# A gated cross-attention and expert layer: the first two groups' k, q and v ahead of the slots, and the order inside a slot

## The chip, the cores and the metric

One core of a Trainium2 chip runs the whole kernel. The metric is the device time of one execution in microseconds (us); lower is better. PE is TensorE, DVE is VectorE, ACT is ScalarE, POOL is GpSimd, SP is SyncE, which only issues DMAs here.

## The reference, cut to what matters

```python
def reference(x, ctx, g_xattn, g_ffn, wq, wk, wv, Wr, br, W1, b1, W2, b2):
    # x (64, 128, 128), ctx (64, 77, 128); 16 heads of depth 8; 8 experts of width 256
    def xattn(q, k, v):
        Q, K, V = split(q @ wq.T), split(k @ wk.T), split(v @ wv.T)
        attn = softmax(einsum('bhqd,bhkd->bhqk', Q, K) / sqrt(8))
        return merge(einsum('bhqk,bhkd->bhqd', attn, V))
    def ffn(x):
        logits = x @ Wr + br
        gates = softmax(where(one of the two largest, logits, -inf))
        h = relu(einsum('btd,edh->bteh', x, W1) + b1)
        return einsum('bte,bteh,ehd->btd', gates, h, W2) + gates @ b2
    x = x + tanh(g_xattn) * xattn(layernorm(x), ctx, ctx)
    return x + tanh(g_ffn) * ffn(layernorm(x))
```

The two layer norms have no weights. Only the two chosen experts of a row count.

## The kernel before, in words

Each engine has a program of its own, written out by hand; semaphores (`wait_ge`, `then_inc`) order the engines among each other, and within an engine the order of the program is the order of the work. The program is a loop over **slots** `t` = 0 to 103, and in slot `t` each engine does a piece for several sequences that are at different stages. There are 64 sequences `b` in 16 groups `g` of four (`NB` = 4); `u` = `t` // 4 and `r` = `t` % 4 are the slot's group and its place in it.

- **The group chain** makes k, q and v of group `u - 1`, one piece a slot. DVE takes statistics of a sequence's x in slot `t` (`stats1_of`, `mean_var1`), adds eps (`var_eps1`, r = 3), POOL raises to the power -1/2 (`rstd1_of`, r = 0), DVE normalises four tiles (`normed1`, r = 1). PE projects k (r = 0), turns the normalised x (r = 1), projects q (r = 2) and v (r = 3), each into one PSUM bank, `group_bank`. ACT copies each result out (`k_high`, `turned_x1`, `q_high`, `v_columns`); of k and q the copy is the bf16 high half, and DVE subtracts it for the low half (`k_low`, `q_low`). SP stores the halves to DRAM and reads them back in another layout, into the stacks `k_st` and `q_st` (`store_k`, `stack_k`, `store_q`, `stack_q`), with which a product of two bf16 halves takes one matmul. The stacks are cleared beforehand, stack 0 by POOL, 1 and 2 by ACT (`clear_k`). With `turn_x2` the same bank also serves the second layer norm's rows.
- **Maxima**, sequence `t - 8`: for each of four blocks of heads, `h` = 0 to 3, PE computes scores into a bank (`max_scores`) and DVE reduces them to the negative maximum (`head_max`). The first four sequences use four banks that are still free, all others one bank, `max_bank`. Two sequences' maxima are turned on PE (`turn_max`), stored and stacked as a row of `q_st` (`store_max`, `stack_max`), so that the scores come out with the maximum subtracted.
- **Attention**, sequence `t - 13`: PE computes scores in two alternating banks (`scores`), ACT the exponent (`exp_scores`), PE the products with v (`values`, with a column of ones for the sum); in the next slot (sequence `t - 14`) ACT copies out the bank (`output_rows`), PE turns it (`turn_o`) and DVE divides, adds to x and takes the second statistics.
- **Experts.** Rows of x are routed (`route`, then small DVE steps spread over slots), scattered by POOL to DRAM in the order of their experts, read back as **quads** of four tiles, and run through their experts on PE: `hidden_part` in two halves into `hidden_bank`, ReLU on ACT, `rows_out` one slot later, then stored, gathered and added. The slots of the 38 quads are worked out by the program; those that meet the attention are 43 to 50, 55 to 62, 67 to 73 and 75, and the maxima end in slot 71. From slot 78 on there is no attention, only experts. The last eight sequences go through all experts (`dense_units`). The weights w1 are kept as f32; their high halves are read in place as every second bf16 (`upper`), the low halves are a tensor of their own (`w1_lo`), made in slots 33 and 34 by DVE.

PE's order in a slot is that of its `slot` function. In front of the slots PE only waits for the weights and the identity.

## Time and profile before

| | us |
|---|---|
| median of 3 runs | 648.16 |
| lowest and highest | 643.82 and 649.1 |
| span of the profiled execution | 693.9 |
| PE, DVE, ACT, POOL busy in it | 579.1, 374.7, 363.7, 265.3 |
| mean granted TensorE clock, as a share of full speed | 0.925 |

The profile tells no device time of its execution beside the span, so the trace's durations are in the time of a 693.9 us execution. A busy PE is not PE at its peak, since matmuls overlap and their ends are modelled; DMA issues and waits are not counted as busy.

### The profile page before, as it was taken

What the parts mean: (1) busy time and instruction counts of PE and PEld (TensorE: products, weight loads), DVE (VectorE), ACT (ScalarE), POOL (GpSimd) and SP (SyncE); (2) the same over time, 40 slices, a digit from 0 to 9 for tenths busy, and PEclk for the clock granted to TensorE, in tenths of its full rate; (3) what the DMA queues carried; (4) which work ended last, traced back from release to release, by engine and by line L of the source; (5) the groups of instructions that cost most, each with busy time, mean ns of one, the idle gap of its engine ahead of it and who ended that gap; (6) DMA issues with size and microseconds to landing.
All of it is one profiled execution on the core that took longest, in us unless ns stands there. A gap on an engine that the chain in (4) does not pass through costs nothing.

```text
span 693.9 us, 18476 instructions
## 1 busy us (share of the span) xinstructions
PE 579.1 (83%) x6201; PEld 412.4 (59%) x6213; DVE 374.7 (54%) x1361; ACT 363.7 (52%) x835; POOL 265.3 (38%) x281
## 2 busy tenths in 40 slices
PE   2459998989787999899789899788886788899877
PEld 0225555555455566666467667466664587778656
DVE  4455876688655765445765554665543331242354
ACT  5216765655455466666456656455555345456222
POOL 6020010100554002443544435544455255566660
PEclk9968998988788899999999999899999689999999
DMA  4445644544433376664676654553332245764221
GB/s 116 118 115 148 159 107 126 137 105 119 142 95 112 73 118 104 148 103 138 104 132 115 147 109 139 97 125 83 97 107 81 70 98 136 133 148 128 77 77 49
DMA packets 158121, 78.65 MB, mean 113 GB/s; under 512 B 85088, under 2 KB 153312, under 8 KB 158032
## 3 DMA queue, kind: packets, MB, share of 16 engines
q1 hardware_dynamic: 119760, 45.65, 30.4%
q0 software_dynamic: 7168, 14.69, 8.9%
q10 hardware_dynamic: 31104, 17.13, 8.9%
q8 instruction: 54, 0.88, 0.5%
q14 instruction: 35, 0.29, 0.2%
HBM read 30.72 MB, written 36.75 MB: 97 GB/s over the span
## 4 chain that ended last, share of the span: by engine, by line
PE 65%; issue 9%; DMA 7%; DVE 7%; ACT 7%; another core or an unknown queue 2%; POOL 1%; ACTq 1%; SPq 1%; DVEq 0%; POOLq 0%
PE y L607 11%; PE bank_oT L517 9%; PE scores L503 8%; PE max_scores L482 5%; DMA q_st<-q_dram 4%; PE hidden_p L591 4%; PE o L530 3%; PE hidden_p L592 3%; PE hidden_p L593 3%; DVE neg_max L1028 3%; ACT probs L744 2%; PE max_scores L541 2%; PE bank_oT L648 2%; ACT hidden L810 2%
## 5 line engine op out<-in xcount | busy, mean ns | idle before, releaser
L1028 DVE TENSOR_REDUCE neg_max<-max_scores 128x4 f32<-128x308 f32 x244 | 116.2, 476 | 158.7 <-PE max_scores L482 149.4
L744 ACT ACTIVATE probs<-scores 77x512 f32<-77x512 f32 x256 | 148.8, 596 | 69.9 <-PE scores L503 64.2
L1351 POOL DMA_INDIRECT xs_dram<-rows,at x112 | 110.1, 983 | 92.6 <-PE max_scores L482 57.4
L1366 POOL DMA_INDIRECT back<-ys_dram,at x112 | 107.8, 963 | 90.4 <-PE max_scores L482 35.9
L517 PE MATMUL bank_oT<-probs,v_cols 77*9 77x128 f32 x2048 | 110.0, 291 | 13.6 <-ACT probs L744 8.6
L503 PE MATMUL scores<-q_st,k_st 128*77 128x128 bf16 x1024 | 111.7, 236 | 0.1
L482 PE MATMUL max_scores<-k_st,q_st 128*128 128x308 bf16 x244 | 78.8, 323 | 34.9 <-DVE neg_max L1028 12.3
L503 PEld LDWEIGHTS scores<-q_st,k_st 128*77 128x77 bf16 x1024 | 76.5, 124 | 50.8 <-issue 43.7
L810 ACT ACTIVATE hidden<-hidden_p,b_cols 128x128 f32<-128x128 f32 x256 | 73.5, 369 | 54.3 <-PE hidden_p L593 43.3
L607 PE MATMUL y<-w_sb,hidden 128*128 x608 | 96.8, 299 | 0.0
L607 PEld LDWEIGHTS y<-w_sb,hidden 128*128 128x128 f32 x608 | 84.7, 201 | 2.7
L517 PEld LDWEIGHTS bank_oT<-probs,v_cols 77*9 77x9 f32 x2048 | 30.8, 89 | 59.8 <-issue 28.1
L591 PE MATMUL hidden_p<-xsT,w_sb 128*128 128x128 bf16 x256 | 53.5, 228 | 15.2 <-ACT hidden L810 10.7
L819 ACT COPY ys<-y 128x512 f32<-128x512 f32 x38 | 22.3, 588 | 82.1 <-PE y L607 66.0
L1312 POOL TENSOR_TENSOR rstd<-ve,power 128x4 f32<-128x4 f32 x16 | 17.7, 1107 | 114.2 <-DVE ve L996 114.2
L1306 POOL TENSOR_TENSOR rstd<-ve,power 128x4 f32<-128x4 f32 x16 | 16.4, 1027 | 113.3 <-DVE ve L969 90.8
L593 PE MATMUL hidden_p<-xsT,w_sb 128*128 128x128 bf16 x256 | 52.7, 222 | 0.3 <-issue 0.3
L592 PE MATMUL hidden_p<-xsT,w_lo 128*128 128x128 bf16 x256 | 52.6, 222 | 0.0
L482 PEld LDWEIGHTS max_scores<-k_st,q_st 128*128 128x128 bf16 x244 | 25.1, 103 | 45.6 <-DVE neg_max L1028 20.8
L738 ACT COPY oT<-bank_oT 128x512 f32<-128x512 f32 x64 | 37.6, 587 | 22.2 <-PE bank_oT L517 15.1
L530 PE MATMUL o<-ident,oT 128*128 128x128 f32 x256 | 43.2, 296 | 5.9 <-ACT oT L738 5.9
L591 PEld LDWEIGHTS hidden_p<-xsT,w_sb 128*128 x256 | 25.2, 99 | 32.1 <-issue 27.4
...
## 6 DMA issues: line engine op xcount, KB each, us to landing
...
```

The source lines that it names most:

```text
L482: mm(max_to(b, h)[:, 0:PER * KEYS], q_st[g % 3][:, h, seq_cut(b, S)], k_st[g % 3][:, h, b % NB, :, :].rearrange("p j k -> p (j k)"), start ...
L503: last = mm(score_bank[h % 2][0:KEYS, j * S:(j + 1) * S], k_st[g % 3][:, h, b % NB, j, :], q_st[g % 3][:, h, seq_cut(b, S)], start=True, s ...
L517: last = mm(oT_bank[ROWS * j:ROWS * j + VW, h * S:(h + 1) * S], v_cols[g % 3][:, b % NB, h * PER + j, :], probs[h][:, j * S:(j + 1) * S], ...
L591: mm(o, w_hi[:, at_w], tiles[:, 0, cut], start=True, stop=False, skip_group_check=True)
L592: mm(o, w1_lo[:, at_w], tiles[:, 0, cut], start=False, stop=False, skip_group_check=True)
L593: last = mm(o, w_hi[:, at_w], tiles[:, 1, cut], start=False, stop=True, skip_group_check=True)
L607: last = mm(o, hidden[:, (2 * q + t // 2) % 4, t % 2, m, :], w2_sb[:, bass.ds(w + m * 128, 128)], start=False, stop=(m == HC - 1), skip_gr ...
L744: nc.scalar.activation(probs[h][:], score_bank[h % 2][0:KEYS, :], ACT.Exp, scale=SCALE).then_inc(s_exp, 1)
L810: last = nc.scalar.activation(hidden[:, k % 4, i, m, :], of[:, j * 128:(j + 1) * 128], ACT.Relu, bias=b1_cols[:, bass.ds(held[q][2 * half ...
L1028: V.tensor_reduce(neg_max[:, i // 2, :, h, i % 2], max_to(b, h)[:, 0:PER * KEYS].rearrange("p (j k) -> p j k", j=PER), AXIS_X, ALU.max, ne ...
L1351: G.indirect_dma_start(out=xs_dram[c % 2], out_offset=bass.IndirectOffsetOnAxis(ap=at[k][c % 4][:, i:i + 1], axis=0), in_=rows[c % 2][:, i ...
L1366: G.indirect_dma_start(out=back[k][:, b % 16, :], out_offset=None, in_=ys_dram[c % 2][0:TILES[c] * 128, :], in_offset=bass.IndirectOffsetO ...
```

## The change

**Ahead of the slots.** The chains of groups 0 and 1 stand in front of the loop, on every engine, and the loop begins with slot 8. Group 1 works in `hidden_bank` (`work_bank`). SP loads x of groups 2 and 3 and the context of group 2 there too, and stores and stacks in the order k0, k1 stored, k0 stacked, q0 stored, q0 stacked, k1 stacked, q1 stored, q1 stacked. Of `k_st[1]` ACT clears one of four blocks and POOL the rest; POOL also clears `k_st[2]`. The two loads of the gates are issued after `k_high`.

**The other groups' chain** stands one slot earlier: k at r = 3, x turned at r = 0, q at r = 1, v at r = 2; statistics are taken of tile `t + 1`. SP stacks k and stores q at r = 1 and stacks q at r = 2, in front of `store_max`.

**The slot.** On PE the fourth head block's values move into the next slot, behind its first scores; scores 0 and 1 stand before maximum 0, maximum 1 before the first hidden part, and `turn_o` and the route later. ACT copies `output_rows` behind the first exponent, and a quad's first ReLU behind the second. On DVE `heads_normed` stands behind the third maximum.

**Odd maxima.** From sequence 4 on, `h` = 1 and 3 go to `hidden_bank` in every slot without a quad (`lent`); a maximum waits for the reduction of the one before it in its own bank (`max_before`).

**w1.** POOL copies the high halves of w1 to a bf16 tensor of their own in slots 31 and 33; the matmuls and the split read that.

The diff, cut to its core, engine by engine. 
Which bank a maximum uses and what it waits for:

```diff
+def lent(b, h):
+    return h % 2 == 1 and b >= NB and not quads_at(b + MAX_LAG)
+
 def max_to(b, h):
-    return (max_bank, score_bank[0], score_bank[1], y_bank)[h] if b < NB else max_bank
+    if b < NB:
+        return (max_bank, score_bank[0], score_bank[1], y_bank)[h]
+    return hidden_bank if lent(b, h) else max_bank
+
+def max_before(b, h):
+    if b < NB:
+        return HG * (b - 1) + h + 1
+    n = HG * b + h - 1
+    while n >= HG * NB and lent(n // HG, n % HG) != lent(b, h):
+        n -= 1
+    if n >= HG * NB:
+        return n + 1
+    return 0 if lent(b, h) else HG * (NB - 1) + 1
+
+def lent_before(s):
+    return max([HG * b + h + 1 for b in range(clip(s - MAX_LAG, B)) for h in range(HG) if lent(b, h)], default=0)
```

SP, `stack_k`, the slot and what stands ahead of the slots:

```diff
         if g < 3:
-            if g == 0:
-                sp.wait_ge(s_kzero0, 1)
-            else:
-                sp.wait_ge(s_kzero, g)
+            sp.wait_ge(s_kzero, g + 1)
+            if g == 1:
+                sp.wait_ge(s_kzero_part, 1)
...
-        if r == 0 and group_on(u - 1):
-            store_k(u - 1)
...
-        if r == 1 and group_on(u - 1):
+        if r == 1 and later_group(u - 1):
...
+            store_q(u - 1)
+        if r == 2 and later_group(u - 1):
+            stack_q(u - 1)
...
-        if r == 2 and group_on(u - 1):
-            store_q(u - 1)
...
-        if r == 2 and u >= 2 and group_on(u):
-            load_ctx(u)
...
-        if r == 3 and group_on(u - 1):
-            stack_q(u - 1)
+        if r == 3 and later_group(u):
+            store_k(u)
+        if r == 3 and group_on(u + 1):
+            load_ctx(u + 1)
...
+    load_x(2)
+    store_k(0)
+    store_k(1)
+    stack_k(0)
+    store_q(0)
+    load_x(3)
+    stack_q(0)
+    stack_k(1)
+    store_q(1)
+    load_ctx(2)
+    stack_q(1)
```

PE, `max_scores`, `hidden_part`, the slot and what stands ahead:

```diff
-        n = HG * b + h + 1 - (HG if b < NB else 1)
-        if n > 0:
-            pe.wait_ge(s_max, n)
+        if max_before(b, h) > 0:
+            pe.wait_ge(s_max, max_before(b, h))
+        if lent(b, h) and quads_before(b + MAX_LAG):
+            pe.wait_ge(s_relu, 2 * quads_before(b + MAX_LAG))
...
+        if half == 0 and lent_before(QUAD_AT[q]):
+            pe.wait_ge(s_max, lent_before(QUAD_AT[q]))
...
         mx, sc, ob = t - MAX_LAG, t - SCORE_LAG, t - OUT_LAG
         for q in quads_at(t):
             name_weights(q)
+        if active(sc):
+            scores(sc, 0)
+        if active(ob):
+            values(ob, 3)
+        if active(sc):
+            scores(sc, 1)
+        if active(mx):
+            max_scores(mx, 0)
         if r == 0 and group_on(u - 3):
             turn_max(u - 3, 1)
         if r == 2 and group_on(u - 2):
             turn_max(u - 2, 0)
-        if active(sc):
-            scores(sc, 0)
+        if r == 3 and later_group(u):
+            project_k(u)
+        if r == 1 and later_group(u - 1):
+            project_q(u - 1)
         if active(mx):
-            max_scores(mx, 0)
-        if r == 0 and group_on(u - 1):
-            project_k(u - 1)
-        if r == 2 and group_on(u - 1):
-            project_q(u - 1)
+            max_scores(mx, 1)
         for n in dense_at(t):
             dense_units(n)
         for q in quads_at(t):
             hidden_part(q, 0)
         if active(sc):
-            scores(sc, 1)
+            scores(sc, 2)
+        if r == 0 and group_on(u - 5):
+            route(u - 5, t)
         if active(mx):
-            max_scores(mx, 1)
+            max_scores(mx, 2)
+        if active(sc):
+            values(sc, 0)
         if active(ob):
             turn_o(ob, t)
-        if r == 0 and group_on(u - 5):
-            route(u - 5, t)
         for q in quads_at(t - 1):
             rows_out(q, 0)
         if active(sc):
-            values(sc, 0)
-            scores(sc, 2)
-        if active(mx):
-            max_scores(mx, 2)
+            scores(sc, 3)
+            values(sc, 1)
+        if r == 0 and later_group(u - 1):
+            turn_x1(u - 1)
+        if r == 2 and later_group(u - 1):
+            project_v(u - 1)
         for q in quads_at(t - 1):
             rows_out(q, 1)
-        if r == 1 and group_on(u - 1):
-            turn_x1(u - 1)
-        if r == 3 and group_on(u - 1):
-            project_v(u - 1)
-        if active(sc):
-            values(sc, 1)
-            scores(sc, 3)
         if active(mx):
             max_scores(mx, 3)
         if active(sc):
...
-        if active(sc):
-            values(sc, 3)
...
+    project_k(0)
+    project_k(1)
...
+    turn_x1(0)
+    project_q(0)
+    turn_x1(1)
+    project_q(1)
+    project_v(0)
+    project_v(1)
```

ACT, the slot and what stands ahead:

```diff
         if t in (16, 17, 18):
             b2_part(t - 16)
+        if active(sc):
+            exp_scores(sc, 0)
+        for q in quads_at(t - 2):
+            store_y(q)
+        if active(ob):
+            output_rows(ob)
         if r == 0 and group_on(u - 3):
             turned_max(u - 3, 1)
         if r == 2 and group_on(u - 2):
             turned_max(u - 2, 0)
-        if active(ob):
-            output_rows(ob)
-        for q in quads_at(t - 2):
-            store_y(q)
         for n in dense_at(t):
             dense_relu(n)
         if active(sc):
-            exp_scores(sc, 0)
-        if r == 0 and group_on(u - 1):
-            k_high(u - 1)
-        if r == 2 and group_on(u - 1):
+            exp_scores(sc, 1)
+        if r == 3 and later_group(u):
+            k_high(u)
+        if r == 1 and later_group(u - 1):
             q_high(u - 1)
         for q in quads_at(t):
             name_biases(q)
             relu(q, 0)
         if active(sc):
-            exp_scores(sc, 1)
+            exp_scores(sc, 2)
         for q in quads_at(t - 1):
             outputs(q)
-        if active(sc):
-            exp_scores(sc, 2)
-        if r == 1 and group_on(u - 1):
+        if r == 0 and later_group(u - 1):
             turned_x1(u - 1)
-        if r == 3 and group_on(u - 1):
+        if r == 2 and later_group(u - 1):
             v_columns(u - 1)
         if active(sc):
             exp_scores(sc, 3)
...
-    act.dma_start(gates_in[:, 0:1], g_xattn.partition_broadcast(128)).then_inc(s_gin, 16)
-    act.dma_start(gates_in[:, 1:2], g_ffn.partition_broadcast(128)).then_inc(s_gin, 16)
-    clear_k(1)
+    clear_part_of_k(1)
...
+    k_high(0)
+    k_high(1)
+    act.dma_start(gates_in[:, 0:1], g_xattn.partition_broadcast(128)).then_inc(s_gin, 16)
+    act.dma_start(gates_in[:, 1:2], g_ffn.partition_broadcast(128)).then_inc(s_gin, 16)
+    turned_x1(0)
+    q_high(0)
...
+    turned_x1(1)
+    q_high(1)
...
+    v_columns(0)
+    v_columns(1)
```

DVE, the slot and what stands ahead:

```diff
         sums = [b for b in range(SB) if SUM_AT[b] == t]
         if active(mx):
             head_max(mx, 0)
-        if r == 1 and group_on(u - 1):
+        if r == 0 and later_group(u - 1):
             normed1(u - 1)
-        if r == 0 and 0 <= u - 5 < G0:
+        if r == 2 and 0 <= u - 5 < G0:
             rows_low(u - 5)
         if r == 0 and G0 <= u - 5 < NG:
             dense_rows_low(u - 5)
-        if active(t):
-            stats1_of(t)
+        if active(t + 1):
+            stats1_of(t + 1)
         if active(mx):
             head_max(mx, 1)
         if r == 3 and group_on(u - 4):
             normed2(u - 4)
-        if r == 0 and group_on(u - 1):
-            k_low(u - 1)
-        if r == 2 and group_on(u - 1):
+        if r == 3 and later_group(u):
+            k_low(u)
+        if r == 1 and later_group(u - 1):
             q_low(u - 1)
         if r == 0 and group_on(u - 5):
             make_logits(u - 5)
+        if active(mx):
+            head_max(mx, 2)
+        if active(t + 1):
+            mean_var1(t + 1)
         if active(ob):
             heads_normed(ob)
-        if active(mx):
-            head_max(mx, 2)
-        if active(t):
-            mean_var1(t)
         if active(ob):
             add_attention(ob)
             stats2_of(ob)
...
-        if r == 3 and group_on(u):
+        if r == 2 and later_group(u):
...
+    for b in range(NB):
+        stats1_of(b)
+        mean_var1(b)
+    var_eps1(0)
+    k_low(0)
+    normed1(0)
+    k_low(1)
+    for b in range(NB, 2 * NB):
+        stats1_of(b)
+        mean_var1(b)
+    var_eps1(1)
+    q_low(0)
+    normed1(1)
...
+    stats1_of(2 * NB)
+    mean_var1(2 * NB)
+    q_low(1)
```

POOL, the new function, the slot and what stands ahead:

```diff
+    def high_experts(part):
+        half = slice(part * (E * HID // 2), (part + 1) * (E * HID // 2))
+        pool.wait_ge(s_w, 16 * 8)
+        G.tensor_copy(w1_hi[:, half], upper(w1_sb[:])[:, half]).then_inc(s_whi, 1)
+
...
-        if r == 0 and group_on(u - 1):
-            rstd1_of(u - 1)
+        if r == 3 and later_group(u):
+            rstd1_of(u)
...
+        if t in (31, 33):
+            high_experts((t - 31) // 2)
...
-    G.memset(k_st[0][:], 0.0).then_inc(s_kzero0, 1)
+    G.memset(power[:], -0.5).then_inc(s_power, 1)
+    G.memset(k_st[0][:], 0.0).then_inc(s_kzero, 1)
...
+    pool.wait_ge(s_power, 1)
+    rstd1_of(0)
...
-    G.memset(power[:], -0.5).then_inc(s_power, 1)
+    G.memset(k_st[1][:, 1:HG], 0.0).then_inc(s_kzero, 1)
+    rstd1_of(1)
+    for t in v_cols:
+        G.memset(t[:, :, :, DEPTH], 1.0).then_inc(s_fill, 1)
...
-    for t in v_cols:
-        G.memset(t[:, :, :, DEPTH], 1.0).then_inc(s_fill, 1)
-    pool.wait_ge(s_power, 1)
-    pool.wait_ge(s_fill, 4)
+    pool.wait_ge(s_fill, 7)
...
+    G.memset(k_st[2][:], 0.0).then_inc(s_kzero, 1)
```

## Rows read from the trace of the kernel before

**Rows 1.** The page, its first part: busy time, share of the span, instructions.
```profile
PE 579.1 (83%) x6201; PEld 412.4 (59%) x6213; DVE 374.7 (54%) x1361; ACT 363.7 (52%) x835; POOL 265.3 (38%) x281
```

**Rows 2.** Stages: busy time and count by engine, granted clock, DMA share, GB/s.
```profile
26.30:48.95 22.65, 12.15 (x41) 5.71 (x42) 12.40 (x41) 3.11 (x7) 4.77 (x3) 0.82 0.41 103
48.95:67.09 18.14, 17.12 (x181) 9.68 (x179) 11.13 (x39) 10.35 (x19) 0.27 (x1) 0.76 0.54 141
67.09:134.37 67.28, 61.57 (x755) 37.96 (x755) 49.51 (x184) 45.69 (x87) 6.42 (x7) 0.95 0.52 135
134.37:243.04 108.67, 92.05 (x974) 56.95 (x974) 75.89 (x283) 54.35 (x107) 32.27 (x32) 0.81 0.41 106
243.04:317.96 74.92, 68.75 (x845) 51.84 (x841) 38.96 (x142) 47.37 (x124) 24.77 (x25) 1.00 0.66 123
317.96:347.09 29.13, 24.46 (x292) 16.07 (x288) 20.34 (x78) 15.64 (x34) 13.23 (x14) 0.94 0.52 109
347.09:423.63 76.54, 69.29 (x845) 51.87 (x841) 43.95 (x159) 46.98 (x123) 36.02 (x37) 1.00 0.63 127
423.63:455.57 31.94, 25.96 (x292) 16.59 (x288) 20.11 (x74) 15.52 (x34) 17.50 (x18) 0.86 0.55 121
455.57:520.01 64.44, 57.64 (x711) 43.39 (x708) 35.38 (x129) 38.23 (x101) 29.54 (x30) 0.99 0.40 99
```

**Rows 3.** The same view, two stretches of four slots each.
```profile
87.27:109.30 22.03, 20.04 (x256) 12.46 (x255) 16.71 (x62) 14.52 (x29) 2.01 (x3) 1.00 0.52 137
109.30:134.37 25.07, 22.65 (x255) 14.05 (x255) 16.80 (x62) 14.71 (x29) 2.01 (x3) 0.86 0.49 123
```

**Rows 4.** Timeline, two maxima of slot 15: start, duration, instruction, idle before.
```profile
61.92 0.29 PE L482 MATMUL max_scores<-k_st,q_st 128*128 128x308 bf16 x1
62.05 0.39 PE L503 MATMUL scores<-q_st,k_st 128*77 128x128 bf16 x4
62.26 0.48 DVE L1028 TENSOR_REDUCE neg_max<-max_scores 128x4 f32<-128x308 f32 x1 [0.43 <-PE max_scores L482]
62.79 0.30 PE L482 MATMUL max_scores<-k_st,q_st 128*128 128x308 bf16 x1 [0.35 <-DVE neg_max L1028]
```

**Rows 5.** Timeline of PE's weight loads, a part of slot 23.
```profile
105.95 0.93 PEld L458 LDWEIGHTS group<-w_att,ctx_in 128*77 128x77 f32 x8
...
107.05 0.12 PEld L517 LDWEIGHTS bank_oT<-probs,v_cols 77*9 77x9 f32 x8 [0.16 <-issue]
...
107.38 0.26 PEld L503 LDWEIGHTS scores<-q_st,k_st 128*77 128x77 bf16 x4 [0.22 <-issue]
...
107.59 0.10 PEld L482 LDWEIGHTS max_scores<-k_st,q_st 128*128 128x128 bf16 x1
```

**Rows 6.** Timeline of PE, the first hidden part of slot 45.
```profile
261.90 0.23 PE L591 MATMUL hidden_p<-xsT,w_sb 128*128 128x128 bf16 x1 [0.72 <-ACT hidden L810]
```

**Rows 7.** Timeline, the opening.
```profile
1.86 4.20 POOL L1397 MEMSET k_st<- 128x4928 bf16 x1
...
6.93 3.18 DVE L969 TENSOR_SCALAR ve<-mv 128x4 f32<-128x4 f32 x1
...
14.30 4.30 ACT L724 COPY k_st<-zeros_b 128x4928 bf16<-128x4928 bf16 x1
...
26.30 0.44 PE L482 MATMUL max_scores<-k_st,q_st 128*128 128x308 bf16 x1 [4.44 <-DMA q_st<-q_dram]
```

**Rows 8.** Timeline of PE, a maximum of slot 35.
```profile
184.90 0.44 PE L482 MATMUL max_scores<-k_st,q_st 128*128 128x308 bf16 x1 [2.58 <-issue]
```

**Rows 9.** Groups by line: shapes, count, busy us, mean ns, idle before.
```profile
L744 ACT ACTIVATE probs<-scores 77x512 f32<-77x512 f32 x256 | 148.8, 596 | 69.9 <-PE scores L503 64.2 <-remote 4.2
...
L530 PE MATMUL o<-ident,oT 128*128 128x128 f32 x256 | 43.2, 296 | 5.9 <-ACT oT L738 5.9
...
L591 PEld LDWEIGHTS hidden_p<-xsT,w_sb 128*128 x256 | 25.2, 99 | 32.1 <-issue 27.4
...
L592 PEld LDWEIGHTS hidden_p<-xsT,w_lo 128*128 x256 | 25.2, 98 | 2.2 <-issue 0.6
```

57 lines of the change are left out of this document (31 added, 26 removed).

## The prediction

> **What bounds the kernel now.** I read the page first, then the time in stages, then single slots. By the page PE is busy 83% of the span [rows 1], and no other engine comes near, so the question in each stage is what keeps PE waiting. The stages are cut at the first scores of a slot: opening up to slot 12 (26.30 us until slot 8, then 22.65), slots 13 to 15, 16 to 27, 28 to 42, then by turns the stretches with expert quads (slots 43 to 50, 55 to 62, 67 to 73) and without (51 to 54, 63 to 66), and the tail from 520.01 us on [rows 2]. A slot takes 67.28/12 = 5.61 us in 16 to 27, 108.67/15 = 7.24 in 28 to 42, and 74.92/8 = 9.37 in the first quad stretch.
>
> What should a slot without a quad take? On PE, scores of a head take 0.21 us to the next weight load, values 0.33, one large piece of a group's chain 1.10 [rows 5]; a maximum holds PE for 0.13 (62.05 less 61.92) [rows 4]; the four turns of the output take 43.2/64 = 0.68 [rows 9]. That is 4 x (0.21 + 0.33 + 0.13) + 0.68 + about 1.1 = 4.5 us (an estimate: the group's pieces are not equal). DVE is busy 49.51/12 = 4.13 us a slot in 16 to 27 and 75.89/15 = 5.06 in 28 to 42 [rows 2]. So both engines need less than the slot has. The reader sees why at 62 us: a maximum starts at 61.92 and the next at 62.79, after PE waited for the reduction, since one bank holds the maxima [rows 4]. The reduction itself is 0.48 us [rows 4]. That loop of 0.87 us runs through most of such a slot. On top of it the clock was granted at 0.81 of full speed in slots 28 to 42 [rows 2], that is, at the lower of its levels (1.2 GHz, against 2.4) for 0.38 of the time. Slots 20 to 23 and 24 to 27, four each with the same work, give its price: 22.03 us at clock 1.00, and 25.07 at 0.86 [rows 3]; 3.04 us for 0.28 x 25.07 = 7.0 us at the low level, 0.43 us per us.
>
> The timed runs have a median of 648.16 us, the profiled execution a span of 693.9 with no own device time beside it. I make the sum in the trace's time and scale it by 648.16/693.9 = 0.934.
>
> **The opening.** Before, the chain of group 0 ends at 26.30, when q lands [rows 7], and that of group 1 stands in the slots, where slots 8 to 12 take 22.65 us for twenty maxima of 0.48 [rows 2, 4], as slot 12 waits for q again. After, group 1 follows group 0 at once, in the experts' bank, and slots 8 to 11 hold maxima alone. Removed from q's path: the clearing of a k stack on ACT, which stood for 4.30 us between two copies [rows 7]; one quarter of the other stays (1.1 us), the rest goes to POOL: 3/4 of a memset of 4.20 us [rows 7], 3.2 us, and a whole one later. Moved past SP's queue: k of group 1 is stored before k of group 0 is stacked, so stack 0 waits for group 1's chain too; q of 1 is stored and stacked behind k of 1.
>
> POOL's memsets meet DVE. An addition of 128x4 on DVE lasted 3.18 us at 6.93 us, as POOL was filling constants [rows 7]. Whether a normalisation is hurt in the same way no row shows, so both ends are open. If the first normalisation waits out the 3.2 us memset (about 8.8 to 12.0), it ends near 13, as before; if not, near 10.6. The Trainium skill (SBUF — State Buffer, section "SBUF: two separate sides") says that VectorE and GpSimd share a port pair under an exclusive lock, for GpSimd's operation or VectorE's two-port one, and the loser blocks for the whole instruction. The 3.18 us row agrees. By that rule the first normalisation loses the full 2.4 us, and so the rule speaks against this part of the change; without it the opening would end some 3 us sooner than I take.
>
> PE enters slot 8 only after both groups' v, some 27 to 29 us, no sooner than now. But slots 8 to 11 then need only DVE's sixteen reductions (0.48 us each; with statistics of the next tiles 10 us, an estimate), and slot 12 about 3 (four reductions and a normalisation): slot 13 at 40 to 43 instead of 48.95. **I take 42, a gain of 7** (bounds 2 and 12: nothing hidden, or no meeting with POOL). Slots 13 to 15 at 5.2 us instead of 18.14/3 = 6.0: gain 2.5.
>
> **Slots without quads.** Odd maxima get the experts' bank, so a maximum waits for the reduction two before it, and PE does scores, values or a group's piece meanwhile. The 0.35 and like waits go; next late is either PE or DVE. In slots 16 to 27 PE's 4.5 us plus a new wait: values of head 3 now stand second in the next slot, and their exponent stands on ACT behind the copy of turned x (r = 0) or of v (r = 2), which in turn waits for PE. An exponent is 0.60 us [rows 9], the copy, of the same 512 columns, is taken as much; PE does only a maximum, one head's values and scores meanwhile (0.13 + 0.33 + 0.21), so some 0.8 us is waited in two slots of four: 0.4 a slot. That makes 5.0 us, and 12 x (5.61 - 5.0) = **7.3 us**. In slots 28 to 42 DVE's 5.06 is above PE's 4.5: with its waits for the copies of q and k (queued in front of a reduction, as before) I take 5.6, and add 6 us for pauses like that of 2.58 us at 184.90, in which PE waits for nothing that the trace shows and which the change leaves [rows 8]: 108.67 - 15 x 5.6 - 6 = **18.7 us**. Slots 51 to 54 and 63 to 66 now take 29.13 + 31.94 = 61.1 [rows 2]; I take 25.5 each, the outputs of a last quad (2.2) and a pause included: **10 us**. Bounds over all of these: PE's 4.5 and DVE's 5.06 reached without a gap give 13 + 33 + 17 = 63 us; one wait of 0.35 gone from each of the 39 slots in which the bank is lent, and nothing else, 14.
>
> **Chain one slot forward.** q is stacked at r = 2 instead of 3, so a slot's time more until its maxima; its waits after slot 12 are small, so this is counted at 1 us inside the sums above. On SP, stacking q now waits for q's store ahead of the first maxima's store; behind it stand that store, a load of x, its stacking, k's store and the context. The maxima of half 0 have from r = 2 until r = 1 of the next group, three slots or 15 us, for two DMAs of about 4 us each: covered, if the wait for q is under 5 us.
>
> **Quad slots.** The experts hold their bank, so nothing is lent in 21 slots. Here the new order could hurt: maxima 0 and 1 stand close together over one bank, 0.87 us apart at least [rows 4]. But PE waits at this place today: first hidden part after ACT's ReLU, 0.72 us [rows 6]. After, scores 0, values 3, scores 1, maxima 0 and 1 fill this wait (about 1.6 us from the slot's start against ReLU's 1.5 to 1.8). Gain 0.26 a slot where DVE is on time; where it still routes, a loss of up to 1: together **3 us** (bounds 12 and -15).
>
> **Plain high halves.** PE's weight loads of the strided half take 99 ns on average, of the plain low half 98 [rows 9]: removed nothing. Added are two POOL copies of 1024 columns in slots 31 and 33 (1 us at the memset's pace, 2 at twice it), ahead of the first scatter in 34, with DVE's splits in 33 and 34 behind them. POOL has little else there: 0, and 4 us if both copies held DVE. The tail keeps its order: 0.
>
> **Sum.** 7 + 2.5 + 7.3 + 18.7 + 10 + 3 = 48.5 us of 693.9; times 0.934 = 45: **603 us**.
>
> **Rivals.** (1) *DVE takes the bank's place.* If the slots' length is DVE's in-order queue (a reduction behind a normalisation of 1.1 us that waits for POOL, or behind k and q low that wait for ACT), the second bank only moves the wait. For it: 5.06 of 7.24 us busy with such waits. Against: 4.13 of 5.61 in 16 to 27 leaves room. Then the no-quad slots keep half of 36 and the quads lose 4: 7 + 2.5 + 18 - 4 = 24, x 0.934 = 22: 626 us. (2) *All gaps close.* PE is dense enough that the low clock also leaves the opening and slots 28 to 66, and ReLU's wait goes in the quads: 0.43 x 10 more there, 21 x 0.6 = 13 more: 66, x 0.934 = 62: 586. (3) *Slower: PE falls behind DVE in the quad slots.* With reduction 0 late by DVE's tail of the slot before (routing, sums), maximum 1 stalls all of PE with hidden part 0 behind it: up to 0.87 + 0.6 a slot, 21 x 1.47 = 31; if these stalls then bring the low clock into the 216 us of quads (now at 0.99 to 1.00 [rows 2]) for the 0.38 of time seen in slots 28 to 42, 216 x 0.38 x 0.43 = 35 more. 48.5 - 3 - 66 = -20, x 0.934: 667 us. It decides from 45.5/21 = 2.2 us a quad slot on. Against it: today's 0.72 us wait in the same place brought no fall. (4) *It doesn't do what it says*: "ahead" fails in the opening, as PE and SP there stay in the two groups' way, and the lent bank covers 39 of 60 slots only; then the opening gives 2, the no-quad slots 9, and the maxima side by side cost 8 in the quads: 3, and 645 us.
>
> **How the numbers follow.** Chances: forecast 0.55 (own range 590 to 616), (1) 0.18, (2) 0.10, (3) 0.09, (4) 0.08. Likeliest: 603. The range that leaves out 2 in 10 runs from 580 (in (2)'s reach) to 640 (past (1), short of (4) and (3)). A measurement tells about 1% from no change, here 641.7 to 654.6: slower 0.10 from (3), same 0.09 from (4) and the edges of (1), faster 0.81.
>
> **What would show it.** Right: slot 13's first scores near 42 us; PE's waits for the maxima's reduction in slots 16 to 42 almost gone; those stages at about 60 and 90 us; the quad stretches within 3 us of 74.92, 76.54 and 64.44; the tail within 2 us of 173.8. Wrong: a DVE addition or normalisation of over 2 us beside a POOL memset, then a later slot 8 than 29 us; DVE busy over 90% in slots 28 to 42 with PE waiting; hidden part 0 waiting for maximum 1, and clock under 0.95 in a quad stretch.

## The result and the profile after

The changed kernel takes **658.35 us** (median of 4 runs, 650.46 to 659.33) beside 647.32 for the kernel before on the same chip (4 runs, 643.82 to 649.1): a ratio of **1.0149** with a 95% interval of 1.0081 to 1.0218. It is slower by 1.5%; 603 us were predicted.

One thing has to be said ahead of any comparison. The execution of before whose rows stand above was unusually long (span 693.9 us). A second profile of the same kernel (the first experiment) has a span of 646.5 us, like the timed runs, and it is the "before" of all stage comparisons from here on.

The page of the changed kernel, first part, answers to [rows 1]:

```profile
PE 577.8 (88%) x6201; PEld 411.7 (63%) x6213; DVE 382.5 (58%) x1361; ACT 349.5 (53%) x834; POOL 275.7 (42%) x285
```

The time in stages answers to [rows 2]: opening until the first maximum, slots 8 to 12, 13 to 15, 16 to 27, 28 to 42, 43 to 50, 51 to 54, 55 to 62, 63 to 66, 67 to 73, and the rest. Columns: stretch, length, busy time (and count) of PE, weight loads, DVE, ACT, POOL, granted clock, DMA share, GB/s.

```profile
0.00:26.35 26.35, 11.50 (x32) 5.86 (x33) 11.94 (x34) 6.92 (x11) 18.95 (x27) 1.00 0.61 149
26.35:39.66 13.31, 7.35 (x28) 3.63 (x28) 12.62 (x39) 0.95 (x4) 4.75 (x3) 0.79 0.66 157
39.66:55.29 15.63, 15.28 (x171) 9.05 (x169) 9.65 (x32) 9.92 (x20) 1.02 (x1) 0.85 0.59 148
55.29:127.94 72.65, 66.39 (x757) 40.29 (x754) 50.32 (x184) 44.25 (x86) 6.04 (x6) 0.88 0.49 126
127.94:239.13 111.19, 93.91 (x982) 58.56 (x981) 79.02 (x290) 52.82 (x107) 34.47 (x34) 0.82 0.45 114
239.13:312.08 72.95, 69.81 (x848) 52.02 (x844) 39.75 (x142) 45.41 (x123) 23.91 (x25) 1.00 0.52 117
312.08:344.91 32.83, 28.97 (x290) 18.49 (x288) 20.91 (x79) 15.83 (x36) 14.04 (x15) 0.79 0.54 115
344.91:417.88 72.97, 69.79 (x848) 51.91 (x844) 44.54 (x158) 45.64 (x123) 35.52 (x37) 1.00 0.57 125
417.88:450.54 32.66, 29.06 (x291) 18.55 (x288) 20.04 (x70) 15.83 (x36) 17.75 (x19) 0.79 0.52 121
450.54:510.07 59.53, 54.94 (x705) 41.66 (x702) 34.67 (x126) 37.20 (x100) 28.88 (x30) 1.00 0.39 93
510.07:655.84 145.77, 130.84 (x1289) 111.73 (x1298) 59.03 (x214) 74.74 (x195) 90.41 (x94) 0.98 0.48 120
```

The same view of the second profile of before, from slot 16 on:

```profile
67.61:133.81 66.20, 59.01 (x755) 36.40 (x754) 49.38 (x184) 45.45 (x87) 6.40 (x7) 1.00 0.55 137
133.81:230.03 96.22, 84.14 (x974) 51.84 (x973) 75.28 (x282) 54.04 (x107) 31.91 (x32) 0.89 0.47 120
230.03:304.90 74.87, 69.16 (x844) 51.99 (x840) 38.91 (x142) 47.09 (x124) 24.74 (x25) 1.00 0.65 124
304.90:332.70 27.80, 24.48 (x291) 16.11 (x288) 20.21 (x78) 15.56 (x34) 12.88 (x14) 0.94 0.48 102
332.70:409.44 76.74, 70.20 (x845) 52.99 (x841) 43.51 (x158) 47.21 (x124) 36.25 (x37) 0.98 0.65 131
409.44:435.65 26.21, 23.12 (x291) 15.14 (x288) 19.43 (x73) 15.56 (x34) 16.58 (x17) 1.00 0.57 129
435.65:498.40 62.75, 56.68 (x712) 42.84 (x708) 35.83 (x131) 38.25 (x102) 30.42 (x31) 1.00 0.51 108
498.40:646.50 148.10, 134.08 (x1293) 113.47 (x1289) 57.57 (x208) 74.49 (x194) 89.28 (x92) 0.95 0.50 117
```

Read the first column of lengths. Up to slot 15 the change gains 67.61 - 55.29 = 12.3 us. The three quad stretches (74.87, 76.74 and 62.75 before) gain 8.9, the tail 2.3. The four stretches without quads lose: 6.5, 15.0, 5.0 and 6.5, together 32.9 us. That is the result: -12.3 - 8.9 - 2.3 + 32.9 = +9.4, against 655.84 - 646.50 = 9.3.

Now read PE's busy time beside the length in slots 16 to 42. The change makes the two stages 21.4 us longer, but PE stands idle only 23.5 us in them instead of 19.3. PE's busy time has grown by 17.2 us, with the same matmuls, and the granted clock has fallen from 1.00 to 0.88 and from 0.89 to 0.82. So one fifth of the loss is waiting, and four fifths are the same work at the low clock. By the trace the lower level holds for 58.0 us of these two stages, against 20.5 before. So 37.5 us more of it went with 17.2 us more of busy time, 0.46 us per us, near the 0.43 that the prediction took from [rows 3].

What PE waits for in these slots, the view of waits of the changed kernel (who waits for whom: total us, times, longest):

```profile
PE max_scores L580 <- DVE neg_max L1084: 8.1, 5, 2.7
PE scores L542 <- ACT probs L794: 4.1, 2, 2.3
PE o L530 <- DVE nm_hl L1094: 3.4, 8, 0.8
PE max_scores L521 <- DVE logits L1123: 2.3, 6, 0.4
...
PE max_scores L521 <- DVE neg_max L1084: 2.0, 1, 2.0
```

and of the second profile of before:

```profile
PE max_scores L482 <- DVE neg_max L1028: 8.8, 21, 0.9
PE max_scores L482 <- DMA q_st<-q_dram: 3.6, 5, 1.3
```

The maxima's 21 waits for a reduction are gone but for one, as the change means. In their place stands the route (L580) with five waits of up to 2.7 us, and a sixth of 1.3 us for which the view names no releaser. It stands in slots with r = 0. One of them is slot 24; its PE timeline (start, duration, instruction, idle before):

```profile
103.02 0.30 PE L521 MATMUL hidden_p<-k_st,q_st 128*128 128x308 bf16 x1
...
104.83 1.06 PE L580 MATMUL max_scores<-wr_sb,xT 128*128 128x8 f32 x8 [1.29 <-DVE neg_max L1084]
106.27 0.42 PE L521 MATMUL max_scores<-k_st,q_st 128*128 128x308 bf16 x1 [0.38 <-DVE logits L1123]
```

and DVE's of the same time:

```profile
102.70 0.47 DVE L1084 TENSOR_REDUCE neg_max<-max_scores 128x4 f32<-128x308 f32 x1
103.09 1.10 DVE L1032 TENSOR_SCALAR xn<-xs_all,mv,rstd 128x128 f32<-128x128 f32 x4
...
104.32 0.46 DVE L1084 TENSOR_REDUCE neg_max<-hidden_p 128x4 f32<-128x308 f32 x1
105.93 0.19 DVE L1123 TENSOR_TENSOR logits<-max_scores,br_sb 128x32 f32<-128x32 f32 x1 [1.15 <-PE max_scores L580]
```

Maximum 1 is written at 103.02, but DVE first normalises for 1.10 us, and its reduction runs at 104.32. The route waits for that reduction, the logits for the route, maximum 2 for the logits: a chain of PE and DVE in turn, with nothing beside it.

The kernel's text shows one thing more. `route` counts two reductions of its slot (`s_max`, in a function that the change leaves alone). Before, that was the wait for its own bank, as maximum 1 lay in `max_bank` too. In the changed kernel maximum 1 lies in `hidden_bank` in slots without a quad, and the last reduction from the route's bank, reduction 0, ends here at 103.17, 1.66 us before the route starts. So the count holds the route for a bank that it doesn't use. No run tried a smaller count; the logits, which DVE makes behind reduction 1, would still come after it.

Then the clock goes. The stretches of slot 24, before and after 105.90, and slot 25:

```profile
101.18:105.90 4.72, 3.07 (x34) 2.19 (x32) 3.46 (x14) 2.78 (x6) 0.00 (x0) 1.00 0.53 135
105.90:111.03 5.13, 4.76 (x38) 2.63 (x39) 2.39 (x9) 0.69 (x2) 0.00 (x0) 0.50 0.14 29
111.03:117.90 6.87, 6.87 (x63) 3.59 (x59) 3.25 (x11) 3.87 (x7) 0.00 (x0) 0.63 0.56 116
```

The lower level (0.50, that is 1.2 GHz) follows the wait of 1.29 us and lasts into slot 25, so two slots take 16.7 us instead of 7.05 + 5.34 = 12.4 before.

A second place is the slots with r = 2 that follow a routing step. Slot 30, DVE, ACT and PE in the changed kernel:

```profile
144.55 0.24 DVE L1135 TENSOR_REDUCE best<-masked 128x12 f32<-128x96 f32 x1
...
146.40 0.47 DVE L1084 TENSOR_REDUCE neg_max<-max_scores 128x4 f32<-128x308 f32 x1
```

```profile
146.20 0.21 ACT L884 ACTIVATE gap_exp<-gap 128x12 f32<-128x12 f32 x1 [3.15 <-DVE both L1158]
```

```profile
147.35 0.65 PE L542 MATMUL scores<-q_st,k_st 128*77 128x128 bf16 x4 [2.25 <-ACT probs L794]
```

The slot begins on PE at 143.26, while DVE is still in the routing of slot 29 until 146.4. Reduction 0 stands behind it; so does ACT, which waits 3.15 us for the gap of the two best logits and has the exponents queued behind that. PE stands for 2.25 us, and again the clock falls (6.8 of this slot's 10.7 us at 0.50). The one wait for a reduction that is left, 1.98 us in slot 34, is of the same kind: there reduction 0 stands behind a split of w1 and routing steps at the end of slot 33, and the slot takes 8.75 us instead of 5.76.

For the readings below: slots are cut at the first weight load of their scores, and the 35 slots without a quad between 16 and 66 are summed by their place r (9, 9, 9 and 8 of them).

| us | r = 0 | r = 1 | r = 2 | r = 3 | slots 30, 42, 54, 66 |
|---|---|---|---|---|---|
| before, second profile | 57.4 | 57.4 | 50.1 | 51.6 | 25.4 |
| changed | 84.0 | 49.9 | 71.4 | 44.1 | 41.8 |

r = 1 and r = 3 gain 15.0 us, the kind of gain that was forecast; r = 0 and r = 2 lose 47.9. Together that is the loss of 32.9 us from above.

### The profile page after: what moved, and what is told of

Read it like the earlier page. It is cut to its first block, busy times and chain, and to the rows that moved or that the text cites. A ratio compares the mean times of both kernels' runs of the same rounds, so it can differ in the third digit from the quotient of the medians.

```text
span 655.8 us, 18499 instructions
## 1 busy us (share of the span) xinstructions
PE 577.8 (88%) x6201; PEld 411.7 (63%) x6213; DVE 382.5 (58%) x1361; ACT 349.5 (53%) x834; POOL 275.7 (42%) x285
## 4 chain that ended last, share of the span: by engine, by line
PE 70%; DVE 14%; issue 6%; ACT 4%; DMA 3%; ACTq 1%; POOL 1%; SPq 1%; DVEq 0%
PE y L648 12%; PE bank_oT L556 11%; PE scores L542 8%; PE o L569 5%; PE max_scores L521 4%; DVE neg_max L1084 4%; PE group L495 3%; PE hidden_p L632 3%; PE hidden_p L633 3%; PE max_scores L580 3%; PE group L490 2%; ACT probs L794 2%; PE bank_oT L689 2%; PE group L485 2%; PE o L689 2%
## 5 line engine op out<-in xcount | busy, mean ns | idle before, releaser
L1084 DVE TENSOR_REDUCE neg_max<-max_scores 128x4 f32<-128x308 f32 x166 | 78.9, 475 | 86.7 <-PE max_scores L521 86.4
L542 PE MATMUL scores<-q_st,k_st 128*77 128x128 bf16 x1024 | 109.7, 234 | 11.2 <-ACT probs L794 10.7
L542 PEld LDWEIGHTS scores<-q_st,k_st 128*77 128x77 bf16 x1024 | 82.8, 125 | 43.2 <-issue 24.9
L648 PE MATMUL y<-w_sb,hidden 128*128 x608 | 92.4, 290 | 0.0
L860 ACT ACTIVATE hidden<-hidden_p,b_cols 128x128 f32<-128x128 f32 x256 | 73.4, 374 | 25.7 <-PE hidden_p L634 18.3
L648 PEld LDWEIGHTS y<-w_sb,hidden 128*128 128x128 f32 x608 | 81.2, 194 | 1.7
L869 ACT COPY ys<-y 128x512 f32<-128x512 f32 x38 | 22.3, 586 | 84.4 <-PE y L648 84.3
L521 PE MATMUL max_scores<-k_st,q_st 128*128 128x308 bf16 x166 | 52.0, 313 | 15.8 <-DVE neg_max L1084 8.5
L632 PE MATMUL hidden_p<-xsT,w_hi 128*128 128x128 bf16 x256 | 52.5, 226 | 5.1 <-ACT hidden L860 4.6
L1084 DVE TENSOR_REDUCE neg_max<-hidden_p 128x4 f32<-128x308 f32 x78 | 36.8, 472 | 26.7 <-PE hidden_p L521 26.4
L634 PE MATMUL hidden_p<-xsT,w_hi 128*128 128x128 bf16 x256 | 51.3, 221 | 0.0
L569 PE MATMUL o<-ident,oT 128*128 128x128 f32 x256 | 47.1, 312 | 0.7 <-ACT oT L788 0.7
L569 PEld LDWEIGHTS o<-ident,oT 128*128 128x128 f32 x256 | 30.1, 154 | 16.9 <-issue 15.9
L812 ACT COPY xT<-group 128x512 f32<-128x512 f32 x15 | 8.8, 587 | 55.4 <-PE group L485 55.4
```

The costliest lines, as they stand in the source:

```text
L521: mm(max_to(b, h)[:, 0:PER * KEYS], q_st[g % 3][:, h, seq_cut(b, S)], k_st[g % 3][:, h, b % NB, :, :].rearrange("p j k -> p (j k)"), start ...
L542: last = mm(score_bank[h % 2][0:KEYS, j * S:(j + 1) * S], k_st[g % 3][:, h, b % NB, j, :], q_st[g % 3][:, h, seq_cut(b, S)], start=True, s ...
L569: last = nc.tensor.transpose(o_bank[:, h * S:(h + 1) * S], oT[:, h * S:(h + 1) * S], ident[:])
L632: mm(o, w_hi[:, at_w], tiles[:, 0, cut], start=True, stop=False, skip_group_check=True)
L648: last = mm(o, hidden[:, (2 * q + t // 2) % 4, t % 2, m, :], w2_sb[:, bass.ds(w + m * 128, 128)], start=False, stop=(m == HC - 1), skip_gr ...
L860: last = nc.scalar.activation(hidden[:, k % 4, i, m, :], of[:, j * 128:(j + 1) * 128], ACT.Relu, bias=b1_cols[:, bass.ds(held[q][2 * half ...
```

## The experiments

Each was timed beside the kernel before on the same chip; the ratio is to that. In the diffs only the engine's slot function is shown.

**The kernel before, profiled again** (no edit).

> The kernel before, unchanged, with a new profile. Theory: the trace that the prediction rests on was of an execution some 46 us longer than the timed ones (span 693.9 against a median of 647.3), and the surplus is not spread evenly: a new span is 640 to 650 us, with the stretch from slot 75's first scores to the end at 135 to 145 us instead of 166, and the pauses of about 2 us near slots 34 to 38 gone. Rival: the profile always lengthens this kernel, the span is again near 694 and the shortening from 693.9 to 655.8 us is real.

649.79 us, ratio 1.0060 (1.0012 to 1.0109), span 646.5. So two sets of runs of one kernel can differ by over half a per cent with an interval that excludes 1. The longer trace has its extra 47.4 us in three places: slots 28 to 42 (108.67 against 96.22), slots 63 to 66 (31.94 against 26.21) and the tail (173.87 against 148.10), 44 together; slots 16 to 27 and the first two quad stretches agree within 1.1 us. Pauses in which PE waits for nothing visible, like that of [rows 8], make up a part of it (in slots 16 to 42, 7.8 us of such waits, and none over 0.5 us in the second profile). What caused them was not tried.

**The normalisation late, the gap's exponent late, and both.** First: DVE does `normed1` behind the logits instead of ahead of reduction 1.

```diff
         if active(mx):
             head_max(mx, 0)
-        if r == 0 and later_group(u - 1):
-            normed1(u - 1)
...
             make_logits(u - 5)
+        if r == 0 and later_group(u - 1):
+            normed1(u - 1)
         if active(mx):
             head_max(mx, 2)
```

> The changed kernel with one step moved on DVE: at r = 0 the normalisation of four tiles (1.1 us) stands behind maximum 1 and the logits instead of in front of maximum 1. Theory: the slots at r = 0 without a quad grew from 52 to 79 us (eight slots from 20 to 64) because the router on PE now stands in front of maximum 2 and waits for reduction 1, which DVE reaches only behind the normalisation; PE waits 1.3 us there and 0.4 for the logits, and the granted clock then falls to 0.5 for 7 to 10 us. Expected: PE's wait before the router down to about 0.3 us, the eight slots 15 us shorter in sum, 640 to 646 us. Rival: PE's order (router, logits, maximum 2 in one chain) costs this whatever DVE does first: under 4 us of gain, 654 to 658 us.

642.67 us, ratio 0.9951 (0.9910 to 0.9992): 15.7 us less than the changed kernel, as expected. The r = 0 slots fall from 84.0 to 68.9, and the route's wait in slot 24 from 1.29 to 0.35 us. The r = 2 slots keep 68.5.

Second: ACT's exponent of the gap stands one slot later.

```diff
         if active(sc):
             exp_scores(sc, 1)
+        for c in range(NC):
+            if t == ROUTED[c] + 2:
+                gap_exponent(c)
...
-            if t == ROUTED[c] + 1:
-                gap_exponent(c)
```

> The changed kernel with one step moved on ACT: the exponent of the gap between the two best logits stands one slot later, behind the second exponent of the scores, instead of at the end of the slot in which DVE chooses. Theory: it holds ACT for 3 us while DVE is still choosing, exponent 0 comes late, PE waits 2.3 us for it and the clock falls; slots 30, 42, 54 and 66 took 41.8 us against 28.6. Expected: these four at 7 us each, 12 us in sum, 645 to 649 us. Rival: reduction 0 stands behind the same choosing on DVE, so the wait only moves to maximum 2 or the router: under 3 us.

653.78 us, ratio 1.0148 (1.0069 to 1.0228), the ratio of the changed kernel. The four slots fall from 41.8 to 34.7 and not to 28. ACT's wait had covered another: in slot 30 of the kernel with both edits, maximum 2 waits 1.61 us until 141.68. The profile names ACT's exponent there, but the wait in the program is for reduction 0, which stands behind the same routing steps and ends at 141.62.

> Both steps of the two runs before it. If both theories hold and the gains add up: 26 us less than the changed kernel, 630 to 636 us, faster than the kernel before by 2%. If the low clock, and not the waits, makes most of the length and has a cause of its own: 645 us or more.

640.63 us, ratio 0.9955 (0.9921 to 0.9989): nothing beyond the first edit alone. So of my two causes one was right; the other named the wrong engine.

**The route late on PE.** With the normalisation late, and the route behind the output's turns, maximum 2 behind values 1:

```diff
-        if r == 0 and group_on(u - 5):
-            route(u - 5, t)
-        if active(mx):
+        late = r == 0 and group_on(u - 5)
+        if active(mx) and not late:
             max_scores(mx, 2)
...
             turn_o(ob, t)
+        if late:
+            route(u - 5, t)
...
             values(sc, 1)
+        if active(mx) and late:
+            max_scores(mx, 2)
```

> The changed kernel with the normalisation late (as in e1) and, in slots with r = 0, the route behind the output's turns and the maximum 2 behind values 1. Theory: what is left of the r = 0 slots in e1 (nine slots of 7.66 us, against 5.0 with r = 3) is PE's wait for reduction 1 ahead of the route (0.35 us), its wait for the logits ahead of maximum 2 (0.38 us), and the low clock that follows (2.1 us a slot). With the route 1.5 us later on PE both waits go: nine slots at 6.0 to 6.4 us, 12 to 15 us less than e1: 628 to 632 us, clock above 0.95 in slots 16 to 27. Rival: the gap comes from DVE's load in these slots (5.4 us of 7.7) and only moves to maximum 2 or to the turns; the nine slots stay above 7.2 us and the time is 640 to 645.

**628.69 us, ratio 0.9751** (0.9667 to 0.9835), in the expected interval. Slot 24 takes 6.51 us (9.85 in the changed kernel), and its route runs without a wait:

```profile
100.67 0.96 PE L580 MATMUL max_scores<-wr_sb,xT 128*128 128x8 f32 x8
```

The stage view of the two stretches 16 to 27 and 28 to 42:

```profile
55.50:119.20 63.70, 58.70 (x758) 36.64 (x755) 49.87 (x184) 43.96 (x86) 6.05 (x6) 1.00 0.57 144
119.20:216.00 96.80, 84.16 (x983) 52.50 (x981) 77.34 (x288) 52.51 (x107) 34.20 (x33) 0.91 0.49 130
```

PE's busy time is back at 142.9 us (143.2 before, 160.3 in the changed kernel): the 17 us of low clock went with the wait.

The same edit without the normalisation's:

> The changed kernel with the route alone moved (behind the output's turns, maximum 2 behind values 1); the normalisation stays ahead of reduction 1, as the change has it. Theory: what costs is the meeting of the two, the route early on PE and reduction 1 late on DVE; either edit alone takes the wait of 1.3 us away, so this is worth as much as e1 or a little more: nine slots with r = 0 at 62 to 70 us (84.0 in the changed kernel), 634 to 643 us. Rival: the normalisation ahead of reduction 1 is the cause whatever PE's order is, since reductions 1 and 2 stay 1.1 us late: the nine slots stay above 76 us and the time above 648.

632.55 us, ratio 0.9793 (0.9735 to 0.9851); r = 0 slots 61.5, a little better than expected. Of the 26.6 us that the r = 0 slots lost, the normalisation alone brings back 15.1, the route alone 22.5 and both together 24.1. The two don't add, so it is the meeting of an early route and a late reduction that costs. The rival (the normalisation's place alone) falls.

**DVE's routing in the middle of the slot** (with the normalisation late; then with the route late too). The steps of slots with r > 0 stand behind reduction 1, the splits of w1 in slots 34 and 37.

```diff
             normed1(u - 1)
+        if t in (34, 37):
+            split_experts((t - 34) // 3)
+        for c in range(NC):
+            if ROUTED[c] <= t <= PLACED[c] and not (r == 0 or t >= 72):
+                routing_step(c, t - ROUTED[c])
         if active(mx):
             head_max(mx, 2)
...
-        if t in (33, 34):
-            split_experts(t - 33)
         for c in range(NC):
-            if ROUTED[c] <= t <= PLACED[c]:
+            if ROUTED[c] <= t <= PLACED[c] and (r == 0 or t >= 72):
```

> The changed kernel with the normalisation late (as in e1) and DVE's routing steps of slots with r > 0 moved from the end of the slot to behind reduction 1 and the logits, as well as the two splits of w1 (now in slots 34 and 37, at the same place). Theory: in slots with r = 2 reduction 0 stands behind the routing steps of the slot before, and maximum 2 with the exponents behind it; behind reduction 1 the same steps have PE's values, turns, scores and piece of the chain to hide them. Slots 30, 42, 54 and 66 (38.8 us in e1) take 27 to 29, slot 34 (8.8) takes 6, together 12 to 15 us less than e1: 628 to 632 us. Rival: DVE is simply full in these slots (7 us of work), so the steps delay reduction 2 and the output's sums instead: the four slots stay above 35 us, and the time is 640 to 645.

640.65 us, ratio 0.9929 (0.9891 to 0.9967); the four slots take 34.5 us. That is the rival's time, and about its slots.

> Both edits of e4 and e5 (with the normalisation late). Theory: two separate waits, so the gains add: 642.7 less 24 to 30 is 613 to 619 us; the stages 16 to 27, 28 to 42, 51 to 54 and 63 to 66 take 62, 87, 26 and 26. Rival: one queue (DVE) behind both, so that what one edit frees the other takes: no better than the better of the two by more than 4 us, 625 to 640.

627.44 us, ratio 0.9694 (0.9609 to 0.9779): 1 us better than the route alone, so the gains don't add, as the rival has it. The trace shows where DVE's queue holds PE now. In slot 30 PE's turn of the maxima (L530), which stands ahead of maximum 1 and scores 2, waits for DVE's halves, now late behind the moved block:

```profile
135.13 0.24 PE L530 MATMUL o<-ident_b,nm_hl 128*64 128x128 bf16 x1 [1.73 <-DVE nm_hl L1097]
```

**The same block half a slot later than in the changed kernel**, behind reduction 1 of the next slot, and the counts and gates likewise (with the normalisation and the route late, and the splits where the two runs before have them):

```diff
+            for step in {2: (1,), 3: (2, 3), 5: (5,)}.get(t - ROUTED[c], ()):
+                if t < 72:
+                    routing_step(c, step)
...
-            if t == ROUTED[c] + 1:
+            if t == ROUTED[c] + (2 if t < 72 else 1):
                 gap_exponent(c)
```

> As e4 (normalisation and route late), and of DVE's routing the second choice moves from the end of its slot to behind reduction 1 of the next one (slots 30, 42, 54, 66), the gates and the counts behind reduction 1 of the slot after, the gap's exponent on ACT to the end of slots 30, 42, 54, 66, the splits to slots 34 and 37 behind reduction 1. Theory: in e6 these four slots stayed at 37.4 us because the block, one slot sooner, delayed the halves of the maxima, for whose turn PE stands right ahead of maximum 1 (in slot 30 the turned maxima came at 135.4, 3.5 us into the slot). Half a slot later than in e4 nothing of the slot's start waits for the block: the four slots take 25 to 29 us, and the time is 9 to 13 us below e6 (627.4): 614 to 619. Rival: DVE is full in r = 2 (6 to 7.5 us of work in 8 to 10), so reduction 2 and the sums of the output come late, and maximum 0 and the turns of the next slot wait instead: slots 31, 43, 55 and 67 grow by what the four lose, and the time stays at 624 to 632.

623.32 us, ratio 0.9659 (0.9604 to 0.9715). The four slots take 21.9 us, less than before the change (25.4), but the time misses the 614 to 619 that were expected. Slots 43, 55 and 67 grew to 28.5 us together (20.4 with the route late only): the rival held there. In slot 43 the counts put reduction 2 at 216.46, and maximum 3 waits for it:

```profile
216.99 0.44 PE L521 MATMUL max_scores<-k_st,q_st 128*128 128x308 bf16 x1 [1.83 <-DVE neg_max L1087]
```

So the counts go back to the end of their slot:

```diff
-            for step in {2: (1,), 3: (2, 3), 5: (5,)}.get(t - ROUTED[c], ()):
+            for step in {2: (1,), 3: (2,), 5: (5,)}.get(t - ROUTED[c], ()):
...
-            if ROUTED[c] <= t <= PLACED[c] and (r == 0 or t >= 72):
+            if ROUTED[c] <= t <= PLACED[c] and (r in (0, 3) or t >= 72):
```

> As e8, but the counts of the routing (six DVE steps, 143.3 less 141.6 or 1.6 us) go back from behind reduction 1 to the end of slots 31, 43, 55 and 67, where the changed kernel has them; the gates (0.9 us) stay behind reduction 1. Theory: what e8 gave back is that the counts hold reduction 2 of these r = 3 slots (in slot 43 it came at 216.46, and maximum 3 waited 2.24 us on PE): slots 43, 55 and 67 go from 28.5 us together to 21 to 23, slot 32 from 11.9 to 9.5 or 10, and the time falls by 7 to 10 us from 623.3: 613 to 616. Rival: the 1.6 us of DVE work cost the same wherever they stand in r = 3, and the next slot's reduction 0 takes the delay: slots 44, 56 and 68 grow by 1.5 to 2 us each, and the time stays at 620 to 627.

**619.47 us, ratio 0.9593** (0.9539 to 0.9646), the fastest version here, 4.1% below the kernel before. Slots 43, 55 and 67 take 22.1 us, and 44, 56 and 68 didn't grow (29.2 against 29.4), so for these slots the theory holds. The time lies between the theory's and the rival's: the gain is 4 and not 7 to 10 us, and the intervals of this version and the one before overlap. In the profiled execution slot 38 took 2.6 us more and the tail 2. Stages 28 to 42, 51 to 54 and 63 to 66 of this version:

```profile
119.45:213.10 93.65, 83.44 (x983) 52.19 (x981) 76.42 (x282) 52.65 (x106) 32.72 (x33) 0.91 0.50 129
285.82:310.51 24.69, 23.08 (x290) 15.09 (x288) 18.34 (x70) 15.36 (x35) 11.87 (x13) 1.00 0.50 116
382.66:407.28 24.62, 23.14 (x291) 15.13 (x289) 17.69 (x63) 15.28 (x35) 15.92 (x17) 1.00 0.55 134
```

**One bank.** The changed kernel with nothing lent:

```diff
 def lent(b, h):
-    return h % 2 == 1 and b >= NB and not quads_at(b + MAX_LAG)
+    return False
```

> The changed kernel, whole, but no maximum is lent the experts' bank: all maxima from sequence 4 on use one bank again, in the new order. Theory: the second bank pays where DVE is on time (r = 1 and r = 3: 5.5 and 4.9 us a slot, against 6.4 and 5.8 with the one bank of the kernel before) and is not what makes the r = 0 and r = 2 slots longer; without it the neighbouring maxima 0 and 1 wait for a reduction (0.48 us) at least once more in each of the 35 slots without a quad from slot 16 on: 17 to 30 us more than the changed kernel, 675 to 690. Rival (DVE is the bound, the bank is without effect): 655 to 662. Second rival (the bank does the harm, because PE runs ahead into the route and then stands): under 650.

682.90 us, ratio 1.0609 (1.0506 to 1.0712): the second bank is worth some 25 us in the new order. r = 1 and r = 3 slots go from 49.9 and 44.1 to 54.7 and 50.5, and in slots 16 to 42 the maxima wait again:

```profile
PE max_scores L521 <- DVE neg_max L1084: 17.8, 29, 2.4
```

**Plain w1 alone**, on the kernel before:

```diff
-        w_hi = upper(w1_sb[:])
+        w_hi = w1_hi
...
+        if t in (31, 33):
+            high_experts((t - 31) // 2)
```

> The kernel before with the plain high halves of w1 alone (POOL's two copies in slots 31 and 33, the matmuls and the split reading them). Theory: a strided load of weights costs what a plain one does, so this is worth nothing: 0.994 to 1.006 of the kernel before, quad stretches of 74.9, 76.6 and 62.7 us, mean of hidden_part's weight loads 98 to 100 ns. Rival 1: the plain halves are where the 9 us came from that the quad stretches gained: 637 us, quad stretches of 73 to 59. Rival 2: POOL's copies hold DVE ahead of the splits: slots 31 to 34 longer by 2 to 4 us, 649 to 651.

645.96 us, ratio 0.9964 (0.9927 to 1.0001): nothing that these runs tell from 1, seeing that the unchanged kernel came out at 1.006. Neither of the rivals' times fits the interval, the second by little. In the profiled execution (649.03 us) the quad stretches took 73.82, 75.52 and 62.10 us, 2.9 less in all than in the second profile of before. So up to a third of the 8.9 us that the quads gained may be the plain halves or the scatter of single executions.

## Why the prediction was wrong

**The opening: right.** Predicted: slot 8 no sooner than 27 to 29 us, slot 13 at 42, slots 13 to 15 at 5.2 us. Measured: 26.35, 39.66, and 15.63 / 3 = 5.2. The gain, 12.3 us, is more than the 9.5 of the sum mainly because slot 8 begins at 26.35 and not at 27 to 29; slots 8 to 12 take the 13 us that the prediction worked out, and are DVE's work end to end (12.62 busy of 13.31). The open question of [rows 7] is answered by the timeline of POOL and of DVE in the changed kernel:

```profile
8.19 3.17 POOL L1486 MEMSET k_st<- 128x3696 bf16 x1
...
19.33 4.20 POOL L1505 MEMSET k_st<- 128x4928 bf16 x1
```

```profile
9.20 2.82 DVE L1032 TENSOR_SCALAR xn<-xs_all,mv,rstd 128x128 f32<-128x128 f32 x4
...
19.67 0.23 DVE L1012 BATCH_NORM_STATS2 stats<-xs_all 128x6 f32<-128x128 f32 x1
```

The first normalisation took 2.82 us beside the memset and ended at 12.0, against 1.10 in slot 24, a loss of 1.7 us; the first of its four tiles ended at 11.44, 0.08 us behind the memset. The Trainium skill (SBUF — State Buffer, section "SBUF: two separate sides") has GpSimd and some of VectorE's operations, those in a two-port mode among them, share a locked port pair; the trace agrees for the normalisation, while the statistics at 19.67 beside a later memset were not held. Slot 8 began at 26.35 all the same, so this decides nothing.

**Slots without quads: wrong, and this decides.** The step that failed is "The 0.35 and like waits go; next late is either PE or DVE", with the argument against rival (1), "4.13 of 5.61 in 16 to 27 leaves room". The waits did go, but for one, and r = 1 and r = 3 gained 15 us. But room on DVE was read as an average over a stage, and what counts is the order inside a slot at one r. The change moves the normalisation (1.10 us) from r = 1 to r = 0, ahead of reduction 1, where `rows_low` (0.68 us) stood, and the route, which waits for that reduction, now stands ahead of maximum 2, the turns and values 0. The diff shows both; the prediction priced neither, nor the route's count of two reductions. Nor did it name DVE's routing at a slot's end as the thing ahead of reduction 0 outside the quad slots. With these orders mended and the rest of the change kept (the last version above), the stages take 63.6, 93.7, 24.7 and 24.6 us, against 60, 90, 25.5 and 25.5 predicted. That is close only because the prediction's figures stand in the long first trace's time: scaled by 0.934 like the sum, they are 56, 84, 24 and 24, and the mended kernel's 619.47 us are 16 above the forecast. The sum took 36 us (7.3 + 18.7 + 10) from these four stages; measured on the second profile of before, the changed kernel lost 32.9 in them and the mended one gained 9.9.

**The price of the low clock** stood in the prediction (0.43 us per us), but only as a gain that gaps closing would bring (rival 2) and as a loss in quad slots (rival 3). In rival (1), whose mechanism this is, it was left out; there it made four fifths of the loss in slots 16 to 42 and turned half a gain into a loss. Rival (3) had the mechanism whole (DVE's routing makes reduction 0 late, PE stalls, the clock falls) at the wrong place: in the quad slots it didn't happen.

**Quad slots: right in kind, too small.** 8.9 us instead of 3. The wait of [rows 6] is gone in slot 45, and maximum 1 stands there with no wait either:

```profile
258.56 0.29 PE L521 MATMUL max_scores<-k_st,q_st 128*128 128x308 bf16 x1
258.69 0.22 PE L632 MATMUL hidden_p<-xsT,w_hi 128*128 128x128 bf16 x1
```

PE's waits for ReLU in the three stretches fall from 7.3 us to 0.6 (L591 before, L632 now), and its idle time from 18.3 to 10.9. The gain is 0.42 us a slot (8.9/21) instead of 0.26, and the loss that I set against it did not come.

**Plain w1, the tail: right.** The loads, by line as in [rows 9], in the changed kernel:

```profile
L634 PEld LDWEIGHTS hidden_p<-xsT,w_hi 128*128 x256 | 25.1, 98 | 0.0
...
L632 PEld LDWEIGHTS hidden_p<-xsT,w_hi 128*128 x256 | 24.9, 97 | 17.4 <-issue 13.2
```

97 to 98 ns, against 99 for the strided and 98 for the plain half in [rows 9]: nothing. The tail changed by 2.3 us.

**The base.** The sum rested on one execution of 693.9 us and was scaled by 0.934 throughout. Its extra time was not spread evenly but lay in three stages. Slots 28 to 42 took 12.5 us more in it than in the second profile, two thirds of the 18.7 us that I took there; all four stages without quads were 237.0 us in the first trace and 216.4 in the second. And the rows themselves held a bound I passed by: PE is idle 5.7 and 16.6 us in the two stages [rows 2], 22.3 together, and I took 26 from them. That is a bound for an unchanged clock; above it, only a rise of the clock could have paid.

**What stays open:** what lengthened the first trace of before; whether the turn of the maxima (6.2 us of PE's waits in slots 16 to 42 of the fastest version) can be moved too; what a smaller count in `route` would have given; and why the clock falls behind a wait of 0.35 us in one version and not in another (last section).
